# Channel attention: the reciprocal of the softmax sums as ScalarE's exp(-ln) and one Newton step on VectorE

## The chip, the cores and the metric

The kernel runs on one core of one Trainium2 chip. Times are device microseconds (us) of one execution of the whole program. The program is four transformer layers over a batch of 4 sequences of 512 tokens with 128 features. The change touches one stage of the fourth layer, called the channel stage here.

## The reference, cut to the changed stage

For each token, 16 heads take their 64 channels as a sequence of length 64: scores are products of single numbers, a causal mask lies over them, and a softmax runs over the channels. What the change touches is the division inside `softmax`.

```python
Q = (x @ Wq + bq).reshape(b, s, H, C) * inv_sqrt_c        # H = 16, C = 64
K = (x @ Wk + bk).reshape(b, s, H, C)
V = (x @ Wv + bv).reshape(b, s, H, C)
scores = jnp.einsum('bshq,bshk->bshqk', Q, K)
mask = jnp.triu(jnp.ones((C, C), dtype=bool), 1)
scores = jnp.where(mask, -jnp.inf, scores)
w = jax.nn.softmax(scores, axis=-1)
attn = jnp.einsum('bshqk,bshk->bshq', w, V)
return attn.reshape(b, s, HID) @ Wo + bo
```

The result is added to x and normalised, and then goes to a router and to experts.

## The kernel before

A first loop over the 4 sequences does three layers, expert blocks follow, then a second loop over the 4 sequences does the channel stage, and last come the experts of layer four. In the channel stage a sequence is 4 tiles (`tt`, 0 to 3) of 128 tokens. A tile's scores are cut into `NC` = 18 chunks (`c`, 0 to 17) of up to 128x1536 numbers: 6 `early` ones for the upper half of the queries (`half` = 1), then 8 `rect` and 4 `late` ones for the lower half (`half` = 0). All engines walk through the 72 chunks `n` in an order written out by hand, held together by semaphores.

A chunk goes through these steps. GpSimd multiplies queries and keys into one of five buffers `D3` (L1662). VectorE subtracts the maxima (`subtract`, L1712), two chunks ahead of its own `weigh`. ScalarE takes exp in place (L1631). TensorE adds up the numbers over the keys with transposing matmuls into the PSUM bank `psD[half]`, the softmax's denominators (`sum_chunk`, L1530). VectorE multiplies by the values into `W3` (`weigh`, L1726). TensorE adds those up into `psA[half]`, the numerators (L1530 again), one chunk later.

The 8 lowest queries of each head ("own" scores) go another way: ScalarE does them with 128 short exps a tile, 9 or 10 after each chunk from c = 1 to 14 (`own_scores`, L1621). The first of a tile waits until TensorE has finished the last own sums of the tile before, `own_num` (L1539). Their sums come at the end of a tile: TensorE's `own_den` at c = 15 and 16, VectorE's multiplication (L1732) at c = 16 and 17, TensorE's `own_num` at c = 17 and at c = 0 of the next tile.

`finish(tt, half)` on VectorE divides: a reciprocal of `psD[half]` (L1740), then a product with `psA[half]` into `AT` (L1746), 128x512 each. It is called for half 1 at c = 8 of the same tile (`FINISH_1`), and for half 0 at c = 3 of the next tile (`FINISH_0`), or at the stage's end for the last tile. TensorE projects `AT` at c = 6 of the next tile. For tiles 0 to 2, TensorE fills the next tile's keys and queries at c = 8 to 11 (`fill_qk`, L1499 and L1500), and ScalarE moves each part one chunk later (`move_qk`, L1603 and L1607). At c = 12 VectorE scans the next tile's keys (L1685), and the maxima of the next tile follow at c = 14 and c = 0 (L1698 to L1700).

Of the kernel before, what the change touches and what calls it, by code (L numbers as in the profile page):

```python
# [10 lines left out]
ALU = mybir.AluOpType  # L11
ACT = mybir.ActivationFunctionType
# [3 lines left out]
BATCH, T = 4, 512  # L16
NT = T // P
# [48 lines left out]
def transformer(nc, inp, out, last_stage=8):  # L66
    ctx = ExitStack()
    with ctx:
        def sb(name, cols, rows=P, dtype=FP32):
            return ctx.enter_context(nc.sbuf_tensor(name, [rows, cols], dtype))  # L70
# [3 lines left out]
        def sem(name):  # L74
            s = ctx.enter_context(nc.semaphore(name))
            sems.append(s)
            return s
# [20 lines left out]
        wa2 = sb("wa2", 3 * NH * HD)  # L98
# [32 lines left out]
        tab = sb("tab", 2 * BLOCKS_2, dtype=U32)  # L131

        gb, xb = wq1, wk1

        rows_d = nc.dram_tensor("rows_d", ((NE + 1) * REGION, ROW), FP32, kind="Internal").ap()
        y2_d = nc.dram_tensor("y2_d", ((NE + 1) * REGION, P), FP32, kind="Internal").ap()
# [8 lines left out]
        def take(cols):  # L145
            a = arena[:, top[0]:top[0] + cols]
            top[0] += cols
            assert top[0] <= AR + LENT, top[0]
            return a
# [76 lines left out]
        RD = QN  # L226
        AT = [take(NH * HD) for _ in range(2)]
# [9 lines left out]
        rows = take(16)  # L237
# [232 lines left out]
        def route_sems(name):  # L470
# [10 lines left out]
        both = sem("both")  # L481
        pr_ = {k: sem(f"prune_{k}") for k in ("s0", "sc", "ff", "bias", "w", "step")}
        c3 = {k: sem(f"c3_{k}") for k in (
            "d", "e", "w", "den", "num", "attn", "proj", "qk", "qk_sb", "v", "kh", "prod", "chain", "rows",
            "own", "own_den", "own_w", "own_num", "q_ps", "neg")}

        def x_ready(eng, stage):
# [16 lines left out]
        def of_tile(a, i):  # L504
            return a[:, i * P:(i + 1) * P]
# [29 lines left out]
        def back_act(act, j, k, i, bank):  # L535
            n = nrm
            act.wait_ge(n["xps"], NT * j + k + 1)
            nc.scalar.activation(of_tile(xT, i), psum[:, bank, 0:P], ACT.Copy).then_inc(n["xT"], 1)  # L538
# [667 lines left out]
        def scatter_pool(pool, k):  # L1206
            nc.gpsimd.indirect_dma_start(out=rows_d[:, :], out_offset=bass.IndirectOffsetOnAxis(ap=place[:, k:k + 1], axis=0),
                                         in_=xrow[:, k * ROW:(k + 1) * ROW], in_offset=None).then_inc(scattered, 16)
# [226 lines left out]
        psA = [psum[:, 4, :], psum[:, 5, :]]  # L1435
        psD = [psum[:, 6, :], psum[:, 7, :]]
        scratch = psum[:, 2, :]
        HB_ = NH * HD // 2
        NC = len(chunks)
        NALL = NT * NC  # L1440
        EARLY, LATE = len(early), len(early) + len(rect)
# [7 lines left out]
        SCAN, MAX_1 = EARLY + 6, EARLY + 8  # L1449
        V0_AT = NC - 1  # L1450

        SCATTER_AT = {EARLY + k: k for k in range(NT)}
        GATHER_AT = {EARLY + k: k for k in range(PLACES)}

# [5 lines left out]
        PARTS, PART = 4, HD // 4  # L1460
# [21 lines left out]
        def qk_bank(tt, j):  # L1482
            return psum[:, (4, 5, 3, 2)[j], :] if tt == 0 else scratch
# [111 lines left out]
        def channel_act(act):  # L1595
            s = c3

            def move_qk(tt, j):
                dst = (K3, Q3)[j // 2][tt % 2]
                act.wait_ge(s["qk"], 4 * tt + j + 1)  # L1600
                if tt >= 2:
                    act.wait_ge(s["prod"], (tt - 1) * NC)
                nc.scalar.activation(dst[:, j % 2 * 512:j % 2 * 512 + 512], qk_bank(tt, j), ACT.Copy,  # L1603
                                     scale=HD ** -0.5 if j < 2 else 1.0).then_inc(s["qk_sb"], 1)
                if j < 2:
                    by_head = KH[tt % 2].rearrange("p (h c) -> p c h", h=NH)[:, j * HD // 2:(j + 1) * HD // 2, :]
                    nc.scalar.activation(by_head, qk_bank(tt, j).rearrange("p (c h) -> p c h", h=NH), ACT.Copy, scale=HD ** -0.5)\  # L1607
                        .then_inc(s["kh"], 1)

            def own_scores(tt, c):  # L1610

                by_key = EA.rearrange("p (k n) -> p k n", k=HD)
                keys = KH[tt % 2].rearrange("p (h k) -> p h k", h=NH)
                if c == min(OWN_AT):
                    act.wait_ge(s["kh"], 2 * tt + 2)
                    act.wait_ge(s["neg"], tt + 1)
                    if tt > 0:
                        act.wait_ge(s["own_num"], tt * PARTS)
                for r, h in OWN_AT[c]:
                    j = r * NH + h  # L1620
                    nc.scalar.activation(by_key[:, 0:HD - r, j], keys[:, h, 0:HD - r], ACT.Exp, bias=NB[:, j:j + 1],  # L1621
                                         scale=Q3[tt % 2][:, j:j + 1]).then_inc(s["own"], 1)

            for j in range(4):
                move_qk(0, j)
            act.wait_ge(s["qk_sb"], 4)
            for n in range(NALL):
                tt, c = n // NC, n % NC
                cols = chunks[c].cols
                act.wait_ge(s["d"], n + 1)  # L1630
                nc.scalar.activation(D3[n % 5][:, 0:cols], D3[n % 5][:, 0:cols], ACT.Exp).then_inc(s["e"], 1)  # L1631
                if c == Q0_AT and tt + 1 < NT:
                    act.wait_ge(s["qk_sb"], 4 * tt + 8)
                    act.wait_ge(s["d"], (tt + 1) * NC)
                    nc.scalar.activation(psM[0], Q3[(tt + 1) % 2][:, 0:HB_], ACT.Copy).then_inc(s["q_ps"], 1)
                if tt + 1 < NT and c in MOVE_AT:
                    move_qk(tt + 1, MOVE_AT[c])
                if c in OWN_AT:
                    own_scores(tt, c)
                if c == ROWS and tt > 0:  # L1640
                    act.wait_ge(s["proj"], tt)
                    nc.scalar.activation(of_tile(rT, tt - 1), scratch[:, 0:P], ACT.Copy).then_inc(s["rows"], 1)
            for tt in range(NT):
                back_act(act, 1, tt, tt, tt % 2)

        def channel_pool(pool):
            s = c3
            for n in range(NALL):
# [14 lines left out]
                last.then_inc(s["prod"], 1)  # L1663
                if tt == 0 and c in SCATTER_AT:
                    scatter_pool(pool, SCATTER_AT[c])
                if tt == 1 and c in GATHER_AT:
# [3 lines left out]
        def channel_dve(dve):  # L1670
            s = c3
            chain = [0]

            def then(ins):

                chain[0] += 1
                ins.then_inc(s["chain"], 1)
                dve.wait_ge(s["chain"], chain[0])
# [54 lines left out]

            def finish(tt, half):

                done = tt * NC + (EARLY if half == 1 else NC)
                dve.wait_ge(s["den"], done)
                if half == 0:
                    dve.wait_ge(s["own_den"], (tt + 1) * PARTS)
                then(nc.vector.reciprocal(RD, psD[half]))  # L1740
                dve.wait_ge(s["num"], done)
                if half == 0:
                    dve.wait_ge(s["own_num"], (tt + 1) * PARTS)
                if tt >= 2:
                    dve.wait_ge(s["proj"], tt - 1)
                nc.vector.tensor_tensor(AT[tt % 2][:, half * HB_:(half + 1) * HB_], RD, psA[half], ALU.mult)\  # L1746
                    .then_inc(s["attn"], 1)
                dve.wait_ge(s["attn"], 2 * tt + 2 - half)

# [5 lines left out]
            for n in range(NALL):  # L1755
                tt, c = n // NC, n % NC
                if tt > 0:
                    if c == MAX_0:
                        maxima(tt, 0)
                    if c == FINISH_0:  # L1760
                        finish(tt - 1, 0)
                    if c == STATS:
                        dve.wait_ge(s["rows"], tt)
                        stats_dve(dve, 1, tt - 1, tt - 1, of_tile(rT, tt - 1))
                    if c == SCALE:
                        scale_dve(dve, 1, tt - 1, tt - 1, of_tile(rT, tt - 1))
                if c == FINISH_1:
                    finish(tt, 1)
                if tt + 1 < NT:
                    if c == SCAN:  # L1770
                        scan_keys(tt + 1)
                    if c == MAX_1:
                        maxima(tt + 1, 1)
                if n + 2 < NALL:
                    subtract(n + 2)
                weigh(n)
            finish(NT - 1, 0)
            dve.wait_ge(s["proj"], NT)
            stats_dve(dve, 1, NT - 1, NT - 1, scratch[:, 0:P])
# [124 lines left out]
        with nc.Fori(0, BATCH) as b:  # L1904
            with nc.Block() as block:
# [14 lines left out]
                @block.scalar  # L1920
                def _(act):
                    norm_act(act, 0, (3, 4))
                    channel_act(act)
                    route3_act(act)
# [97 lines left out]
```

## Time and profile before

| | us |
|---|---|
| median of 3 runs | 3361.55 |
| lowest, highest | 3359.6, 3368.39 |
| the profiled execution | 3359.82 |
| its span on the core | 3357.6 |

The profile is of one execution. Each instruction has a start, a duration, and, where its engine sat idle before it, the idle time with the instruction that ended it. The four passes of the channel stage lie between 1565 and 3240 us of the span; nearly all that is read here is from the first of them, and the others repeat it. In the tables of the trace PE is TensorE, DVE VectorE, ACT ScalarE and POOL GpSimd.

### The profile page before, as it was taken

What the parts mean: (1) busy time and instruction counts of PE and PEld (TensorE: products, weight loads), DVE (VectorE), ACT (ScalarE), POOL (GpSimd) and SP (SyncE); (2) the same over time, 40 slices, a digit from 0 to 9 for tenths busy, and PEclk for the clock granted to TensorE, in tenths of its full rate; (3) what the DMA queues carried; (4) which work ended last, traced back from release to release, by engine and by line L of the source; (5) the groups of instructions that cost most, each with busy time, mean ns of one, the idle gap of its engine ahead of it and who ended that gap; (6) DMA issues with size and microseconds to landing.
All of it is one profiled execution on the core that took longest, in us unless ns stands there. A gap on an engine that the chain in (4) does not pass through costs nothing. (4 is left out here: it accounts for less than half of the span.)

```text
span 3357.6 us, 53815 instructions
## 1 busy us (share of the span) xinstructions
PE 2734.4 (81%) x19496; PEld 2117.8 (63%) x19496; DVE 2228.7 (66%) x4199; ACT 1853.3 (55%) x4363; POOL 1544.6 (46%) x1473
## 2 busy tenths in 40 slices
PE   1998699869986998596888878888788887788857
PEld 0465546554655575495777766777677776677756
DVE  2167416842683268433999959999599995999943
ACT  0364436543554455422887718877287773877723
POOL 0141214221422241313886618767088761886614
PEclk8999899989998999898999989999799998999988
DMA  9400000000000000093000000000000000000005
GB/s 221 132 1 1 5 10 1 1 5 10 1 1 5 10 1 1 21 332 104 4 7 1 1 5 4 7 1 1 5 4 7 1 1 5 4 7 1 1 19 162
DMA packets 75396, 93.46 MB, mean 28 GB/s; under 512 B 9324, under 2 KB 61339, under 8 KB 74984
## 3 DMA queue, kind: packets, MB, share of 16 engines
q1 hardware_dynamic: 61278, 70.70, 7.5%
q0 software_dynamic: 5184, 10.29, 0.9%
q10 hardware_dynamic: 8650, 8.77, 0.8%
q8 instruction: 167, 2.74, 0.3%
q14 instruction: 117, 0.96, 0.1%
HBM read 61.58 MB, written 28.62 MB: 27 GB/s over the span
## 5 line engine op out<-in xcount | busy, mean ns | idle before, releaser
L1662 POOL TENSOR_TENSOR arena<-arena 128x1536 f32<-128x1536 f32 (+9 forms) x480 | 1024.5, 2161 | 337.0 <-DVE arena L1726 250.1
L1530 PE MATMUL psum<-ident,arena 128*128 128x128 f32 (+7 forms) x7168 | 869.0, 279 | 221.7 <-ACT arena L1631 204.0
L1530 PEld LDWEIGHTS psum<-ident,arena 128*128 128x128 f32 (+7 forms) x7168 | 792.2, 137 | 328.4 <-ACT arena L1631 260.6
L1621 ACT ACTIVATE arena<-arena 128x64 f32<-128x64 f32 (+7 forms) x2048 | 707.7, 484 | 144.1 <-PE psum L1539 144.1
L1726 DVE TENSOR_TENSOR arena<-arena,psum 128x1536 f32<-128x1536 f32 (+9 forms) x480 | 494.3, 1062 | 78.2 <-ACT arena L1631 70.5
L1712 DVE TENSOR_TENSOR arena<-arena,psum 128x1536 f32<-128x1536 f32 (+9 forms) x480 | 493.6, 1061 | 22.6 <-POOL arena L1662 20.7
L894 POOL TENSOR_SCALAR arena<-arena 128x512 f32<-128x512 f32 (+3 forms) x512 | 264.1, 533 | 498.7 <-DVE arena L857 498.6
L1631 ACT ACTIVATE arena<-arena 128x1536 f32<-128x1536 f32 (+2 forms) x288 | 405.7, 1415 | 148.9 <-DVE arena L1712 148.9
L815 ACT ACTIVATE arena<-arena 128x512 f32<-128x512 f32 (+3 forms) x512 | 281.7, 552 | 183.5 <-DVE arena L850 183.5
L517 POOL TENSOR_SCALAR veps<-mv 128x1 f32<-128x1 f32 x112 | 21.5, 192 | 707.7 <-DVE mv L512 703.0
L768 PEld LDWEIGHTS psum<-ident,arena 128*128 128x128 f32 x1280 | 142.1, 144 | 169.5 <-ACT arena L826 83.6
L768 PE MATMUL psum<-ident,arena 128*128 128x128 f32 x1280 | 186.1, 287 | 70.8 <-ACT arena L826 41.7
L1539 PE MATMUL psum<-ident,arena 128*128 128x128 f32 (+7 forms) x2048 | 234.0, 273 | 0.0
L1539 PEld LDWEIGHTS psum<-ident,arena 128*128 128x128 f32 (+7 forms) x2048 | 223.4, 137 | 1.2
L497 PE MATMUL psum<-ident 128*128 128x128 f32 x976 | 143.4, 297 | 65.8 <-issue 39.4
L726 PE MATMUL psum<-arena 64*128 64x256 f32 (+3 forms) x1024 | 187.7, 472 | 10.0 <-DVE arena L850 8.1
L850 DVE CUSTOM_DVE_ANT_0 arena<-psum,cmask 128x384 f32<-128x384 f32 (+3 forms) x256 | 112.0, 488 | 120.0 <-PE psum L726 120.0
L497 PEld LDWEIGHTS psum<-ident 128*128 128x128 f32 x976 | 136.9, 216 | 75.3 <-issue 69.2
L784 PE MATMUL psum<-arena 128*64 128x128 f32 x2560 | 180.5, 282 | 0.4
L538 ACT ACTIVATE xT<-psum 128x128 f32<-128x128 f32 x112 | 29.8, 277 | 241.4 <-PE psum L533 241.4
L784 PEld LDWEIGHTS psum<-arena 128*64 128x64 f32 x2560 | 138.4, 138 | 29.9 <-issue 28.0
L850 DVE CUSTOM_DVE_ANT_0 arena<-psum,arena 128x512 f32<-128x512 f32 (+3 forms) x256 | 112.3, 488 | 53.9 <-PE psum L726 32.6
(265 smaller groups left out, 3796.7 us busy)
## 6 DMA issues: line engine op xcount, KB each, us to landing
arena<-in_L_ffn_W SPq DMA_DIRECT2D x39, 768.0 KB
arena<-in_L_ffn_W SPq DMA_DIRECT2D x23, 514.0 KB
rows_d<-xrow SPq DMA_DIRECT2D x1, 9504.0 KB, 51.0
y_d<-xrow SPq DMA_DIRECT2D x1, 9216.0 KB, 80.5
arena<-rows_d SPq DMA_DIRECT2D x62, 66.0 KB, 3.9
y_d<-arena POOLq DMA_DIRECT2D x39, 64.0 KB, 4.8
arena<-in_L_ffn_h_w ACTq DMA_DIRECT2D x2, 1024.0 KB
wa<-in_L_attn_W_attn ACTq DMA_DIRECT2D x1, 1536.0 KB
```

What stands on the lines that cost most here:

```text
L497: nc.tensor.matmul(psum[:, bank, 0:P], ident[:], ident[:], start=True, stop=True)
L768: last = nc.tensor.transpose(GX[:, half, c:c + P], two(PRG[b % 4])[:, half, c:c + P], ident[:])
L784: last = nc.tensor.matmul(bank[half * HD:(half + 1) * HD, j * P:(j + 1) * P], V[:, c:c + HD], pt[:, half, j * g.n + kt * P:j * g.n + (kt + ...
L815: nc.scalar.activation(pr, pr, ACT.Exp, bias=nb[:, u:u + 1], scale=-1.0, accum_out=rsum[:, u:u + 1]).then_inc(s["probs"], 1)
L894: nc.gpsimd.tensor_scalar(pr, pr, rinv[:, u:u + 1], 1.0, ALU.mult, ALU.mult).then_inc(s["scaled"], 1)
L1530: last = nc.tensor.matmul(ps[ch.half][0:rows, to:to + P], buf[:, c:c + rows], ident[:], start=first, stop=False, is_transpose=True, skip_g ...
L1539: last = nc.tensor.matmul(ps[0][0:rows, 0:P], EA[:, k * NH * OWN:k * NH * OWN + rows], ident[:], start=False, stop=k == HD - 1, is_transpo ...
L1621: nc.scalar.activation(by_key[:, 0:HD - r, j], keys[:, h, 0:HD - r], ACT.Exp, bias=NB[:, j:j + 1], scale=Q3[tt % 2][:, j:j + 1]).then_inc( ...
L1631: nc.scalar.activation(D3[n % 5][:, 0:cols], D3[n % 5][:, 0:cols], ACT.Exp).then_inc(s["e"], 1)
L1662: last = nc.gpsimd.tensor_tensor(of_piece(D3[n % 5], piece), q, keys_on(K3[tt % 2], k, nk, w), ALU.mult)
L1712: last = nc.vector.tensor_tensor(d, d, queries_on(psM[ch.half], ch, piece), ALU.subtract)
L1726: last = nc.vector.tensor_tensor(of_piece(W3[n % 2], piece), of_piece(D3[n % 5], piece), keys_on(psV, k, nk, w), ALU.mult)
```

## The change

ScalarE gets a new step, `seeds(tt, half)`. It waits for the denominators to be complete, writes ln of `psD[half]` (128x512) into a buffer `RS[half]`, which lies in `wa2` (weights of layer three, not used any more), and then exp of minus that in place. For half 1 this stands after the own scores of c = 7 of the same tile (`SEED_1`), for half 0 after the own scores of c = 1 of the next tile (`SEED_0`), and after the last chunk for the last tile. VectorE's `finish` has no reciprocal any more. It waits for the seed r, makes d times r, then (that minus 2) times r, which is the negative of Newton's next value, and takes the sign back in the product with `psA[half]`, which becomes a scalar_tensor_tensor. Nothing else is changed.

```diff
+        SEED_1, SEED_0 = EARLY + 1, 1
...
+            def seeds(tt, half):
+                act.wait_ge(s["den"], tt * NC + (EARLY if half == 1 else NC))
+                if half == 0:
+                    act.wait_ge(s["own_den"], (tt + 1) * PARTS)
+                k = 2 * tt + 2 - half
+                if k >= 3:
+                    act.wait_ge(s["attn"], k - 2)
+                nc.scalar.activation(RS[half], psD[half], ACT.Ln).then_inc(s["ln"], 1)
+                act.wait_ge(s["ln"], k)
+                nc.scalar.activation(RS[half], RS[half], ACT.Exp, scale=-1.0).then_inc(s["seed"], 1)
...
                 if c in OWN_AT:
                     own_scores(tt, c)
+                if c == SEED_1:
+                    seeds(tt, 1)
+                if c == SEED_0 and tt > 0:
+                    seeds(tt - 1, 0)
...
+            seeds(NT - 1, 0)
             for tt in range(NT):
                 back_act(act, 1, tt, tt, tt % 2)
...
             def finish(tt, half):
                 done = tt * NC + (EARLY if half == 1 else NC)
-                dve.wait_ge(s["den"], done)
-                if half == 0:
-                    dve.wait_ge(s["own_den"], (tt + 1) * PARTS)
-                then(nc.vector.reciprocal(RD, psD[half]))
+                dve.wait_ge(s["seed"], 2 * tt + 2 - half)
+                then(nc.vector.tensor_tensor(RD, psD[half], RS[half], ALU.mult))
+                then(nc.vector.scalar_tensor_tensor(RD, RD, -2.0, RS[half], ALU.add, ALU.mult))
                 dve.wait_ge(s["num"], done)
...
-                nc.vector.tensor_tensor(AT[tt % 2][:, half * HB_:(half + 1) * HB_], RD, psA[half], ALU.mult)\
+                nc.vector.scalar_tensor_tensor(AT[tt % 2][:, half * HB_:(half + 1) * HB_], RD, -1.0, psA[half], ALU.mult, ALU.mult)\
                     .then_inc(s["attn"], 1)
```

What the build makes of `seeds` the diff does not tell. This is the order of ScalarE's instructions around c = 7 and 8 of a sequence's first tile, before the change (the 128x1536 rows are the exps of chunks, the short ones own scores):

```order
L1631 ACTIVATE arena<-arena 128x1536
L1621 ACTIVATE arena<-arena 128x61 x10
L1631 ACTIVATE arena<-arena 128x1536
L1621 ACTIVATE arena<-arena 128x60 x9
L1631 ACTIVATE arena<-arena 128x1536
```

And with the change (L1647 and L1624 are the old L1631 and L1621):

```order
L1647 ACTIVATE arena<-arena 128x1536
L1624 ACTIVATE arena<-arena 128x61 x10
L1636 ACT_TABLE_LOAD
L1636 ACTIVATE wa<-psum 128x512
L1638 ACT_TABLE_LOAD
L1638 ACTIVATE wa<-wa 128x512
L1647 ACTIVATE arena<-arena 128x1536
L1624 ACTIVATE arena<-arena 128x60 x9
L1647 ACTIVATE arena<-arena 128x1536
```

Four instructions now stand between the own scores of c = 7 and the exp of c = 8: besides ln and exp two loads of ScalarE's function tables, one ahead of each. The same four stand at all eight places of a sequence.

VectorE's order around c = 8 of the same tile, before (the last row is the `subtract` that follows):

```order
L1726 TENSOR_TENSOR arena<-arena,psum 128x1536
L1740 RECIPROCAL arena<-psum 128x512
L1746 TENSOR_TENSOR arena<-arena,psum 128x512
L1712 TENSOR_TENSOR arena<-arena,psum 128x1536
```

And with the change (L1747 and L1733 are the old L1726 and L1712):

```order
L1747 TENSOR_TENSOR arena<-arena,psum 128x1536
L1760 TENSOR_TENSOR arena<-psum,wa 128x512
L1761 SCALAR_TENSOR_TENSOR arena<-arena,wa 128x512
L1767 SCALAR_TENSOR_TENSOR arena<-arena,psum 128x512
L1733 TENSOR_TENSOR arena<-arena,psum 128x1536
```

Three instructions stand where two stood; no other instruction of VectorE has moved, and TensorE's and GpSimd's orders are as they were.

## Rows read from the trace of the kernel before

**Rows 1.** Busy time of each engine over the span, from the page.
```profile
PE 2734.4 (81%) x19496; PEld 2117.8 (63%) x19496; DVE 2228.7 (66%) x4199; ACT 1853.3 (55%) x4363; POOL 1544.6 (46%) x1473
```

**Rows 2.** Stretches: start:end, length, busy us (x instructions) by engine, granted TensorE clock, DMA share, GB/s.
```profile
1780.30:1827.20 46.90, 39.56 (x291) 31.68 (x289) 40.99 (x41) 46.39 (x107) 35.81 (x15) 1.00 0.00 1
1827.20:1850.00 22.80, 17.27 (x122) 14.97 (x123) 22.70 (x17) 20.36 (x45) 13.73 (x6) 0.93 0.00 1
1850.00:1874.40 24.40, 24.40 (x211) 22.66 (x210) 24.33 (x24) 3.97 (x4) 14.93 (x12) 1.00 0.01 1
```

**Rows 3.** ScalarE in order of time: start, duration, instruction, [idle before <- releaser].
```profile
1780.29 3.15 ACT L1621 ACTIVATE arena<-arena 128x64 f32<-128x64 f32 x9 [12.81 <-PE psum L1539]
...
1806.00 3.44 ACT L1621 ACTIVATE arena<-arena 128x61 f32<-128x61 f32 x10
...
1815.76 0.60 ACT L1603 ACTIVATE arena<-psum 128x512 f32<-128x512 f32 x1 [0.51 <-PE psum L1500]
...
1874.45 3.16 ACT L1621 ACTIVATE arena<-arena 128x64 f32<-128x64 f32 x9 [12.00 <-PE psum L1539]
```

**Rows 4.** VectorE in order of time, second tile to third; last row, the first tile.
```profile
1784.79 1.82 DVE L1726 TENSOR_TENSOR arena<-arena,psum 128x896 f32<-128x896 f32 x2 [1.89 <-ACT arena L1631]
...
1806.12 1.75 DVE L1726 TENSOR_TENSOR arena<-arena,psum 128x1536 f32<-128x1536 f32 x1 [0.78 <-ACT arena L1631]
1807.80 3.35 DVE L1740 RECIPROCAL arena<-psum 128x512 f32<-128x512 f32 x1
...
1821.55 1.75 DVE L1726 TENSOR_TENSOR arena<-arena,psum 128x1536 f32<-128x1536 f32 x1 [0.84 <-ACT arena L1631]
...
1827.20 1.75 DVE L1726 TENSOR_TENSOR arena<-arena,psum 128x1536 f32<-128x1536 f32 x1 [2.23 <-ACT arena L1631]
...
1640.48 1.75 DVE L1726 TENSOR_TENSOR arena<-arena,psum 128x1536 f32<-128x1536 f32 x1 [1.00 <-ACT arena L1631]
```

**Rows 5.** ScalarE around a table load in the first loop, in order of time.
```profile
167.20 2.11 ACT L802 ACTIVATE arena<-psum 128x512 f32<-128x512 f32 x5 [0.26 <-PE psum L708]
169.33 1.28 ACT L815 ACT_TABLE_LOAD   x1
```

**Rows 6.** Groups by line and shape: xcount, busy us, mean ns, idle before.
```profile
L1603 ACT ACTIVATE arena<-psum 128x512 f32<-128x512 f32 x64 | 38.0, 594 | 45.3 <-PE psum L1500 45.2
L1740 DVE RECIPROCAL arena<-psum 128x512 f32<-128x512 f32 x32 | 107.2, 3350 | 0.0
L1746 DVE TENSOR_TENSOR arena<-arena,psum 128x512 f32<-128x512 f32 x32 | 22.0, 687 | 17.8 <-PE psum L1539 16.8
L1056 DVE SCALAR_TENSOR_TENSOR arena<-psum,s,arena 128x512 f32<-128x512 f32 x16 | 12.0, 751 | 22.7 <-PE psum L1009 22.7
```

**Rows 7.** One line of ScalarE: durations in ns, least, median and most.
```profile
L1635 ACT ACTIVATE psum<-arena x12: 574/582/586, 1663.5 to 3123.9; 128x512 f32<-128x512 f32 x12
```

**Rows 8.** TensorE in order of time; first three rows channel stage, last one the first loop.
```profile
1807.15 2.78 PE L1530 MATMUL psum<-ident,arena 128*128 128x128 f32 x24
1810.97 2.84 PE L1530 MATMUL psum<-ident,arena 128*128 128x128 f32 x24 [1.03 <-ACT arena L1631]
...
1827.22 4.51 PE L1530 MATMUL psum<-ident,arena 128*128 128x128 f32 x24 [0.90 <-ACT arena L1631]
...
303.10 1.97 PE L768 MATMUL psum<-ident,arena 128*128 128x128 f32 x8 [3.46 <-POOL arena L894]
```

**Rows 9.** Two stretches, columns as in rows 2: after that 3.46 us wait, and inside the 4.51.
```profile
303.10:305.10 2.00, 2.00 (x10) 1.67 (x10) 1.90 (x5) 0.02 (x1) 0.62 (x1) 0.50 0.00 0
...
1828.00:1829.00 1.00, 1.00 (x7) 1.00 (x6) 1.00 (x2) 1.00 (x5) 0.00 (x0) 0.50 0.00 0
```

**Rows 10.** The stage's end in the first sequence: TensorE's last own_den; VectorE's last finish.
```profile
1945.37 3.66 PE L1539 MATMUL psum<-ident,arena 128*128 128x128 f32 x32
...
1951.72 3.35 DVE L1740 RECIPROCAL arena<-psum 128x512 f32<-128x512 f32 x1
1959.28 0.69 DVE L1746 TENSOR_TENSOR arena<-arena,psum 128x512 f32<-128x512 f32 x1 [4.21 <-PE psum L1539]
```

More of the change, by code:

```diff
@@ L133, in transformer @@
         gb, xb = wq1, wk1
+        RS = [wa2[:, 4 * T + j * T:4 * T + (j + 1) * T] for j in range(2)]
         rows_d = nc.dram_tensor("rows_d", ((NE + 1) * REGION, ROW), FP32, kind="Internal").ap()
@@ L483, in transformer @@
         c3 = {k: sem(f"c3_{k}") for k in (
-            "d", "e", "w", "den", "num", "attn", "proj", "qk", "qk_sb", "v", "kh", "prod", "chain", "rows",
+            "d", "e", "w", "den", "num", "attn", "proj", "seed", "ln", "qk", "qk_sb", "v", "kh", "prod", "chain", "rows",
             "own", "own_den", "own_w", "own_num", "q_ps", "neg")}
```

## The prediction, made before the changed kernel ran

> **What bounds the kernel now.** I read the busy times first, then stretches of one tile, then each engine in order of time. Over the span TensorE leads with 81% and VectorE has 66%, ScalarE 55% [rows 1], which would make a move of work from VectorE to ScalarE look right. The span is not one stage, though. One tile of the channel stage runs from the first own score at 1780.29 to that of the next tile at 1874.45, 94.2 us [rows 3]. Its three stretches differ [rows 2]. In the first 46.9 us ScalarE is busy 46.39, VectorE 40.99. In the next 22.8 VectorE is busy 22.70. In the last 24.4 TensorE (24.40) and VectorE (24.33) are full and ScalarE has 3.97.
>
> The loop that closes around a tile is this. Own scores wait for the last `own_num` of the tile before (12.0 and 12.8 us of idle ScalarE) [rows 3]; from there ScalarE runs exps and own scores without a pause but for 0.51 us, and VectorE's `weigh` waits for it again and again, 1.89, 0.78, 0.84 and 2.23 us [rows 4]. The last of these, at 1827.20, is chunk 11. After it VectorE has scans, maxima and own products and never waits again before the tile ends. So a tile costs ScalarE's time up to the exp of chunk 11, then VectorE's and TensorE's time. What ScalarE is given between c = 1 and c = 11 lengthens the tile by all of it; what VectorE is spared there turns into more waiting. Both seeds (c = 1 and c = 7) and both finishes (c = 3 and c = 8) lie in that stretch.
>
> **The removed work.** A finish is 3.35 + 0.69 = 4.04 us now [rows 6]. Afterwards it is a product, two scalar_tensor_tensor, each 128x512: 0.69 by the product's row and 0.75 by the nearest scalar_tensor_tensor's [rows 6], about 2.2 us. VectorE is spared 1.9 us, 32 times, 59 us in all. At the stage's end the reciprocal is already covered: after it VectorE waits 4.21 us for TensorE's sums [rows 10]. Elsewhere VectorE waits for ScalarE right after a finish's neighbours [rows 4]. I take 0 for the gain. Were this cover gone, it would be at most 59 us.
>
> **The added work on ScalarE.** The order has four instructions per seed. A table load took 1.28 us, starting 0.02 after the end of five ACTIVATEs run together [rows 5]. Ln reads a PSUM bank into SBUF like L1603, 0.594 us, and exp of 128x512 is near L1635's 0.582 [rows 6, 7]. Two neighbouring ACTIVATEs overlap by about 0.1 us and a load takes that away once, which adds 0.1, and the gaps are 4 x 0.02. Sum: 2 x 1.28 + 0.594 + 0.582 + 0.1 + 0.08 - 0.1 (exp overlaps its successor) = 3.82 us. Bounds: 3.6 if gaps and overlaps vanish, 4.1 if the chained exp needs 0.3 for its semaphore; the second load stands ahead of that wait and covers it, so I take 3.82.
>
> How many of the 8 seeds of a sequence lie on the path: in the first tile `weigh` of chunk 11 also waits for ScalarE (1.00 us [rows 4]), so its seed counts; tiles two, three and four have two each. That is 7. The last stands behind the last chunk: TensorE's `own_den` ends at 1949.0, the seed would be ready near 1952.9, VectorE ends its own product at 1951.7 and its last product cannot start before 1959.3 [rows 10]. Hidden, with 4.9 us to spare after the two Newton steps. So 4 x 7 x 3.82 = 107 us.
>
> Of a table load the Trainium skill ("ScalarE: Activation LUTs", "What ACT_TABLE_LOAD costs") says that a switch also drains the engine for 1.38 us, 2.66 in all. The row has no such gap; by the page the sum would be 28 x 2 x 1.38 = 77 us larger. The row is the nearer witness. The same page ("Table sets: the hidden batching unit") says that ln followed by exp costs one load, as one set holds both. By that rule a seed would cost 2.5 us and the sum 70 us. The order of this build has two loads, so the rule does not hold here.
>
> **The added wait on TensorE.** Behind a seed stand the exp of c = 8 (or c = 2), and `move_qk`. TensorE waits 1.03 us for the exp of c = 8 now [rows 8] and would wait 4.85. After a wait of 3.46 us in the first loop the granted clock was 0.50, the 1.2 GHz level, and 8 matmuls took 1.97 us [rows 8, 9]. In the channel stage the clock also falls now and then: the 24 matmuls of a chunk's two sums took 4.51 us instead of 2.84, with the clock at 0.50 inside [rows 8, 9]. If it falls behind the seed of c = 7, these 24 matmuls are late by 4.51 - 2.84 = 1.67 us; `fill_qk` stands behind them, and ScalarE, which already waits 0.51 us for it [rows 3], waits that much longer. It has keys and queries to move in tiles one to three, so 4 x 3 x 1.67 = 20 us. Bounds: 0, if the clock holds or other dips go away in exchange; 28 x 1.67 = 47 if every seed pays it. At c = 2 there is no move and VectorE has the spared 1.9 us in hand, so I take 20.
>
> **The sum.** 3359.82 + 107 + 20 = 3487 us. The profiled execution is 1.7 us under the median of 3361.55, less than runs differ among themselves, so I predict 3488 for the median. A difference of 0.3%, 10 us, is about what a measurement of this kernel tells from none.
>
> **Rivals.**
> (a) The clock costs nothing: 3359.8 + 107 = 3467. For it: the 28 seeds hold TensorE up at moments where its work is short, and dips that exist today may only move. Against it: a wait as long as the new ones was followed by a low clock.
> (b) The clock costs more: up to 3359.8 + 107 + 47 = 3514, and 3530 if the 2.1 us of `fill_qk` also run slow some of the times.
> (c) Faster: VectorE is the bound of the stage and ScalarE has room. Then 28 finishes give 28 x 1.9 = 53 us, 3307. It decides when ScalarE's free time in the stretch of the seeds reaches 3.8 us for each. The stage as a whole speaks for it (VectorE full for 47 of 94 us), the first stretch against it: ScalarE idles 0.51 us of 46.9 there [rows 2, 3].
> (d) Each load holds ScalarE for 2.7 us: ACTIVATEs in flight, more of them than in rows 5, must first leave. 107 + 28 x 2 x 1.38 = 184, so 3544 (3564 with the clock). That is the Trainium skill's drain, above. Rows 5 speak against it. With rows alone, a load after a busy engine is seen at 0.02 us of delay.
> (e) The loads are not both executed at full price, or half the delay is made good in the tile's second half, where fewer waits meet: 107 x 2/3 = 71, about 3431.
>
> **How the numbers follow.** Forecast with the clock term near 20 (3478 to 3500): 0.42. (a) 0.23. (b) 0.17. (c) 0.04. (d) 0.06. (e) 0.07, and 0.01 for seeds that are nearly hidden, without change. The range 3450 to 3530 takes in the forecast, (a) and (b), 0.82, and the 3.6 to 4.1 us of a seed (28 x 0.25 = 7 us either way). Leaving out (c), (d), (e) and no change leaves out 0.18. Faster by over 0.3%: 0.04. Within: 0.01. Slower: 0.95.
>
> **What the profile of the changed kernel would show.** ScalarE: 64 table loads more, at 1.28 us, and nothing but the four instructions between the own scores of c = 7 and the exp of c = 8, with 3.8 us from the one to the other. VectorE: three instructions near 0.7 us per finish, a wait for the seed before the one at c = 8 of about 5 us, and more idle time ahead of `weigh` in the first half of a tile. A tile of 94.2 us would be near 102 and, with the clock, 103.5. The second and third stretches of rows 2 would keep their lengths. TensorE: waits near 5 us after a seed, the clock below 1.00 behind them, and a `move_qk` at c = 9 that waits 2 us, not 0.5. I would be wrong if gaps stood around the loads (d), if ScalarE still idled before the tile's first own score by less than now by the amount of the seeds (c, e), or if the tile's tail grew.

## The result and the profile after

The changed kernel takes 3485.73 us (median of 4 runs, 3482.72 to 3490.45), against 3362.65 us for the kernel before. The ratio is 1.0362, with a 95% interval of 1.0343 to 1.0382: 3.6% slower. The forecast was 3488 us.

The engines' busy times, from the page of the changed kernel, to be set beside [rows 1]:

```profile
PE 2783.9 (80%) x19496; PEld 2165.3 (62%) x19496; DVE 2197.6 (63%) x4231; ACT 1976.5 (57%) x4491; POOL 1546.0 (44%) x1473
```

VectorE's busy time fell by 31.1 us and ScalarE's rose by 123.2. The span rose from 3357.6 to 3481.0, 123.4 us, nearly the same as ScalarE's 123.2. That the two agree to 0.2 us is partly luck: four of the 32 seeds do not lengthen the kernel, and other waits make up for them, as is added up further down.

Three stretches of the first sequence's third tile (start:end, length, busy us and instructions by engine, granted TensorE clock, DMA share, GB/s), cut at the same places as those of [rows 2]: from the first own score to the `weigh` of chunk 11 (at 1855.03), then to the late chunks, then to the next tile's first own score (at 1902.27).

```profile
1797.40:1855.00 57.60, 44.75 (x291) 36.76 (x289) 38.88 (x44) 54.05 (x115) 37.28 (x18) 0.88 0.00 1
1855.00:1877.80 22.80, 17.25 (x122) 14.95 (x123) 22.67 (x17) 20.37 (x45) 13.65 (x6) 0.93 0.00 1
1877.80:1902.20 24.40, 24.40 (x211) 22.66 (x209) 24.33 (x24) 3.98 (x4) 14.94 (x12) 1.00 0.01 1
```

The first stretch grew from 46.9 to 57.6 us. VectorE is busy for 38.9 us of it, where it was busy for 41.0, and the clock, 1.00 before, is 0.88. The two later stretches kept their lengths, 22.8 and 24.4 us, so the whole growth of the tile, 10.7 us, lies ahead of the `weigh` of chunk 11: two seeds of 3.9 us, and 2.9 us more of waiting at c = 9. ScalarE in order of time over the same tile (start, duration, instruction, idle before and its releaser), to be set beside [rows 3]:

```profile
1797.40 3.17 ACT L1624 ACTIVATE arena<-arena 128x64 f32<-128x64 f32 x9 [11.21 <-PE psum L1542]
...
1827.01 3.45 ACT L1624 ACTIVATE arena<-arena 128x61 f32<-128x61 f32 x10
1830.48 1.28 ACT L1636 ACT_TABLE_LOAD   x1
1831.78 0.60 ACT L1636 ACTIVATE wa<-psum 128x512 f32<-128x512 f32 x1
1832.39 1.28 ACT L1638 ACT_TABLE_LOAD   x1
1833.69 0.63 ACT L1638 ACTIVATE wa<-wa 128x512 f32<-128x512 f32 x1
1834.22 0.26 ACT L1662 ACTIVATE rT<-psum 128x128 f32<-128x128 f32 x1
...
1843.61 0.60 ACT L1606 ACTIVATE arena<-psum 128x512 f32<-128x512 f32 x1 [3.43 <-PE psum L1503]
...
1902.27 3.15 ACT L1624 ACTIVATE arena<-arena 128x64 f32<-128x64 f32 x9 [12.01 <-PE psum L1542]
```

The tile takes 104.9 us where it took 94.2 (the same tile in [rows 3]), the one before it 102.6 where it took 93.3. This tile is the longest of its kind: in the other three passes the third tile takes 102.5 to 102.7 us. A seed lasts from 1830.46, the end of the own scores, to 1834.32, and as its neighbours would have overlapped without it, it costs a little more: from the start of a block of nine own scores to the exp after it are 6.92 us with a seed between them (1797.40 to 1804.32) and 2.98 without (1805.70 to 1808.68), so 3.9. The fourth tile, which has two seeds and nothing to move, tells the same: from its first own score to the exp of chunk 11 it took 42.1 us (1874.45 to 1916.58) and takes 50.0 (1902.27 to 1952.23), 7.8 us more in each of the four passes. The wait of `move_qk` at c = 9 is 3.43 us, not 0.51. The last seed of a sequence is hidden, as its load starts after 11.34 us of idle ScalarE.

TensorE behind the seed of c = 7 of the second tile, and the clock there:

```profile
1733.36 4.16 PE L1533 MATMUL psum<-ident,arena 128*128 128x128 f32 x24 [4.93 <-ACT arena L1647]
```
```profile
1731.80:1736.00 4.20, 2.65 (x13) 2.65 (x14) 4.10 (x4) 4.20 (x11) 2.81 (x2) 0.61 0.05 16
```

It waits 4.93 us (4.85 were expected), and the clock is 0.61 in the mean from 1731.80 to 1736.00, so part of the 24 matmuls ran at the 1.2 GHz level: 4.16 us, not 2.84 [rows 8]. VectorE's three instructions and the moves on ScalarE, grouped by shape:

```profile
L1761 DVE SCALAR_TENSOR_TENSOR arena<-arena,wa 128x512 f32<-128x512 f32 x32 | 45.6, 1426 | 1.1
L1606 ACT ACTIVATE arena<-psum 128x512 f32<-128x512 f32 x64 | 37.9, 591 | 55.4 <-PE psum L1503 55.2
L1760 DVE TENSOR_TENSOR arena<-psum,wa 128x512 f32<-128x512 f32 x32 | 22.0, 688 | 78.2 <-ACT wa L1638 78.2
L1767 DVE SCALAR_TENSOR_TENSOR arena<-arena,psum 128x512 f32<-128x512 f32 x32 | 22.0, 687 | 20.5 <-PE psum L1542 19.6
```

VectorE waits 78.2 us for seeds. One row was not foreseen: the middle instruction of the Newton step, which reads two tiles of SBUF, took 1.43 us in the mean. In 24 of its 32 calls it took 0.69. In the first tile of each sequence it took 5.75 to 5.85, and once more per sequence 1.26 to 1.63.

### The profile page after: what moved, and what is told of

It is laid out like the page before. It is cut to its first block and busy times, and to the rows that moved or that the text cites. A ratio compares the mean times of both kernels' runs of the same rounds, so it can differ in the third digit from the quotient of the medians.

```text
span 3481.0 us, 54005 instructions
## 1 busy us (share of the span) xinstructions
PE 2783.9 (80%) x19496; PEld 2165.3 (62%) x19496; DVE 2197.6 (63%) x4231; ACT 1976.5 (57%) x4491; POOL 1546.0 (44%) x1473
## 5 line engine op out<-in xcount | busy, mean ns | idle before, releaser
L1533 PE MATMUL psum<-ident,arena 128*128 128x128 f32 (+7 forms) x7168 | 915.2, 289 | 296.0 <-ACT arena L1647 278.9
L1533 PEld LDWEIGHTS psum<-ident,arena 128*128 128x128 f32 (+7 forms) x7168 | 838.9, 143 | 401.5 <-ACT arena L1647 330.3
L1624 ACT ACTIVATE arena<-arena 128x64 f32<-128x64 f32 (+7 forms) x2048 | 707.2, 482 | 136.3 <-PE psum L1542 136.3
L1747 DVE TENSOR_TENSOR arena<-arena,psum 128x1536 f32<-128x1536 f32 (+9 forms) x480 | 494.5, 1063 | 150.0 <-ACT arena L1647 121.1
L1733 DVE TENSOR_TENSOR arena<-arena,psum 128x1536 f32<-128x1536 f32 (+9 forms) x480 | 493.7, 1062 | 22.4 <-POOL arena L1683 20.5
L1647 ACT ACTIVATE arena<-arena 128x1536 f32<-128x1536 f32 (+2 forms) x288 | 406.5, 1415 | 158.4 <-DVE arena L1733 158.4
L518 POOL TENSOR_SCALAR veps<-mv 128x1 f32<-128x1 f32 x112 | 21.5, 192 | 711.7 <-DVE mv L513 707.0
L1542 PE MATMUL psum<-ident,arena 128*128 128x128 f32 (+7 forms) x2048 | 234.0, 273 | 0.0
L1542 PEld LDWEIGHTS psum<-ident,arena 128*128 128x128 f32 (+7 forms) x2048 | 223.4, 137 | 1.2
L1753 DVE TENSOR_TENSOR arena<-arena,psum 128x2048 f32<-128x2048 f32 x64 | 143.2, 2278 | 2.9 <-PE psum L1542 2.9
```

Source lines behind the costliest of these rows:

```text
L1533: last = nc.tensor.matmul(ps[ch.half][0:rows, to:to + P], buf[:, c:c + rows], ident[:], start=first, stop=False, is_transpose=True, skip_g ...
L1542: last = nc.tensor.matmul(ps[0][0:rows, 0:P], EA[:, k * NH * OWN:k * NH * OWN + rows], ident[:], start=False, stop=k == HD - 1, is_transpo ...
L1733: last = nc.vector.tensor_tensor(d, d, queries_on(psM[ch.half], ch, piece), ALU.subtract)
L1747: last = nc.vector.tensor_tensor(of_piece(W3[n % 2], piece), of_piece(D3[n % 5], piece), keys_on(psV, k, nk, w), ALU.mult)
```

## The experiments

In the diffs, `-` is the changed kernel unless another is named.

**VectorE's part alone.**

```diff
-                if c == SEED_1:
-                    seeds(tt, 1)
-                if c == SEED_0 and tt > 0:
-                    seeds(tt - 1, 0)
...
-            seeds(NT - 1, 0)
...
-                dve.wait_ge(s["seed"], 2 * tt + 2 - half)
+                dve.wait_ge(s["den"], done)
+                if half == 0:
+                    dve.wait_ge(s["own_den"], (tt + 1) * PARTS)
```

> VectorE's part alone: ScalarE gives no seeds, finish waits for the denominators as before and does the three new instructions on whatever numbers stand in RS (left out: the seed, so the attention output is not the reference's). Theory of the prediction: what VectorE is spared in the first stretch of a tile only becomes waiting for ScalarE, so the time is that of before, 3362 us, within 0.3%. Rival (VectorE is the bound there): 28 finishes shorter by 1.9 us, minus the 24 us by which the changed trace shows the Newton step stretched, so 3309 to 3335 us.

Measured: 1.0088 of before (1.0070 to 1.0106), which is 30 us slower. (The medians, 3391.6 us against 3358.7, differ by 33, but that of this kernel counts one execution of 5112 us, which the ratio leaves out.) Neither theory said so: with nothing added on ScalarE, a step that was to be shorter made the kernel slower. In order of time, VectorE and then GpSimd in the first tile:

```profile
1625.83 0.68 DVE L1757 TENSOR_TENSOR arena<-psum,wa 128x512 f32<-128x512 f32 x1
1626.54 7.93 DVE L1758 SCALAR_TENSOR_TENSOR arena<-arena,wa 128x512 f32<-128x512 f32 x1
1634.51 0.69 DVE L1764 SCALAR_TENSOR_TENSOR arena<-arena,psum 128x512 f32<-128x512 f32 x1
```
```profile
1623.65 10.26 POOL L1678 TENSOR_TENSOR arena<-arena 128x1536 f32<-128x1536 f32 x3
```

The middle instruction ends at 1634.47, 0.56 us after GpSimd's three multiplications end at 1633.91. It starts while one runs and is not served between them. Over the sequence its calls took 7.93, 3.90, 4.20, 3.46, 0.69, 3.46, 0.69 and 0.69 us. The first own score of the second tile comes 131.3 us after the stage's table load where it came 122.3 us after it before, 9.0 us later, and the next two tiles are as long as before. So only the call of the first tile costs time, though the calls of 3.5 to 4.2 us are long too. In the four passes the first tile, from its first own score to that of the second, grew by 8.6, 9.2, 7.4 and 8.0 us, 33 us of the 35 by which the span grew. ScalarE pays for it at c = 10, where it waited 0.90 us before and now waits for TensorE's part of the next keys:

```profile
1645.27 0.60 ACT L1606 ACTIVATE arena<-psum 128x512 f32<-128x512 f32 x1 [6.77 <-PE psum L1503]
```

The instruction between SBUF and PSUM beside the stretched one is never stretched. On this the Trainium skill ("SBUF — State Buffer", "SBUF: two separate sides") says that VectorE and GpSimd share a pair of SBUF ports under an exclusive lock, held for a whole instruction, which VectorE also needs for two SBUF inputs while GpSimd reads SBUF. The trace agrees: 7.93 us beside GpSimd's multiplications, 0.69 us for the same call later in the sequence.

**The same with the product through PSUM.** This takes the suspected cause away.

```diff
-                then(nc.vector.tensor_tensor(RD, psD[half], RS[half], ALU.mult))
-                then(nc.vector.scalar_tensor_tensor(RD, RD, -2.0, RS[half], ALU.add, ALU.mult))
+                then(nc.vector.tensor_tensor(psD[half], psD[half], RS[half], ALU.mult))
+                then(nc.vector.scalar_tensor_tensor(RD, psD[half], -2.0, RS[half], ALU.add, ALU.mult))
```

> VectorE's part alone again, as in the run with the Newton step alone (left out: the seed), but d times r is written back to the PSUM bank, so that the scalar_tensor_tensor reads PSUM and SBUF, not two tiles of SBUF. Theory: the 33 us by which that run was slower are the 3.5 to 7.9 us that this instruction took while GpSimd multiplied; with a PSUM operand it takes 0.69 us each of 32 times and the time is that of before, within 0.3%. Rival 1 (the form with a scalar is stretched whatever it reads): 33 us slower again. Rival 2 (VectorE is the bound and its spared 62 us count): 3300 to 3330.

Measured: 1.0018 (1.0007 to 1.0030). The group by shape:

```profile
L1758 DVE SCALAR_TENSOR_TENSOR arena<-psum,wa 128x512 f32<-128x512 f32 x32 | 22.1, 692 | 1.1
```

No call is stretched and the loss of the run before is gone but for 0.2%, so the stretch was its cause. A finish costs VectorE 63 us less in this kernel: 32 x (4.04 - 2.07), by the two of [rows 6] and three of 0.69, and the time is no better than before. In the tiles two, three and four the way from the first own score to the exp of chunk 11 is as long as before, within 0.1 us (45.4, 45.4 and 42.1 us): VectorE waits instead, 87.5 us in all ahead of its `weigh` of 128x1536, where it was 49.9. That shows directly that VectorE's time in this stretch buys nothing there. In the four first tiles this way became 5.8 us shorter in all, and the rest of these tiles 9.7 us longer: VectorE's scan of the keys, which also reads two tiles of SBUF, took 8.8 to 9.0 us there in place of 6.7, while GpSimd multiplied back to back. The scan as the reason for the 9.7 us was not tested.

**ScalarE's part alone.**

```diff
-                nc.scalar.activation(RS[half], psD[half], ACT.Ln).then_inc(s["ln"], 1)
+                nc.scalar.activation(tiles(RS[half]), ones[:][:, None, :].to_broadcast([P, 4, P]), ACT.Ln).then_inc(s["ln"], 1)
...
-                dve.wait_ge(s["seed"], 2 * tt + 2 - half)
...
+                dve.wait_ge(s["den"], done)
+                if half == 0:
+                    dve.wait_ge(s["own_den"], (tt + 1) * PARTS)
+                then(nc.vector.reciprocal(RD, psD[half]))
...
```

> ScalarE's part alone: table load, ln, table load, exp stand at the eight places, but read a constant from SBUF and nobody reads their result; VectorE does the reciprocal and the product as before. Theory: the whole loss is ScalarE's, 28 x 3.91 = 109 us and the clock's part of about 11, so 3483 us like the changed kernel, within 8 us. Rival (finish's new wait for the seed is what costs, and ScalarE's time alone is partly hidden): clearly less, 3362 to 3440.

Measured: 1.0361 (1.0341 to 1.0382), the ratio of the changed kernel to the third digit. ScalarE's instructions alone make the whole loss. Neither the wait for the seed nor the stretched step adds to it. (Its ln, which reads SBUF, took 0.63 us, not 0.60, which is 1 us in all.)

**One table set.**

```diff
+            nc.scalar.preload_act_table_set("natural_log_exp_and_others")
             for j in range(4):
                 move_qk(0, j)
```

> The changed kernel with one table set that holds exp and ln, loaded once at the start of each sequence's channel stage, so that a seed is ln and exp alone. Theory: a seed falls from 3.91 to about 1.31 us, 28 x 2.6 = 73 us less, and TensorE waits near 2.3 us instead of 4.9 behind it, so the clock's 11 us go too: 3400 us, 3395 to 3415. Rival (the loads are hidden and the wait for the seed is what costs): above 3450.

Measured: 1.0211 (1.0191 to 1.0232), 3431 us. Better than the changed kernel by 1.5% of before, but 30 us short of the forecast. The stretched step is back: 2.88 us in the mean, 7.9 us in a first tile. Without the loads the seed comes earlier, and the step falls into GpSimd's multiplications again. As in the run with the Newton step alone, the first tiles pay: ScalarE waits 5.5 to 6.2 us at c = 10 there.

**One table set and the product through PSUM.** Both edits above.

> The kernel with one table set, loaded once a sequence, and the Newton step through PSUM. Theory: the two causes add up, a seed costs 1.31 us of ScalarE's time and the step no more waits for GpSimd, so 28 x 1.31 = 37 us over before, near 3396 to 3402; against 3431 with the step in SBUF. Rival (the table loads were not the larger part and the rest is the wait for the seed): it stays near 3430.

Measured: 1.0103 (1.0086 to 1.0120), 34.6 us over a before of 3356.18 us, where 28 x 1.31 = 37 was worked out. ScalarE in order of time:

```profile
1625.25 3.45 ACT L1624 ACTIVATE arena<-arena 128x61 f32<-128x61 f32 x10
1628.54 0.58 ACT L1636 ACTIVATE wa<-psum 128x512 f32<-128x512 f32 x1
1629.15 0.63 ACT L1638 ACTIVATE wa<-wa 128x512 f32<-128x512 f32 x1
1629.69 1.47 ACT L1648 ACTIVATE arena<-arena 128x1536 f32<-128x1536 f32 x1
```

From the start of the ten own scores to the exp are 4.44 us, with the loads 7.21 (1620.97 to 1628.18 in the changed kernel). So about 2.8 us of a seed are its loads. Before the change the same way took 3.30 us (1618.43 to 1621.73), so a seed without loads costs about 1.15 us and not 1.31, because it overlaps with its neighbours, and 28 of them cost 32 us. The fourth tile says the same: 44.4 us to the exp of chunk 11, not 42.1, for two seeds. So the sum of 37 was a little high; the 34.6 us are known to about 6, and do not tell the two apart.

**The product through PSUM in the changed kernel.** The same edit, with the seeds and their loads as they are.

> The changed kernel with the Newton step through PSUM and nothing else. Theory: behind the seeds with table loads GpSimd is mostly idle when the step comes, and the one that is stretched per sequence (5.8 us in the first tile) is hidden, so 3478 to 3486, no more than 0.2% under the changed kernel. Rival: the stretched steps cost their 24 us here too: 3460.

Measured: 1.0382 (1.0366 to 1.0398). The time lies in the range of the theory, 3482.9 us, and there is no gain: the ratio is, if anything, above the changed kernel's 1.0362, and the two intervals overlap. The stretch costs nothing where ScalarE is late by more.

**TensorE kept busy behind the seed, twice.**

```diff
+                if c == EARLY + 1:
+                    pe.wait_ge(s["d"], tt * NC + EARLY)
+                    if tt > 0:
+                        pe.wait_ge(s["rows"], tt)
+                    idle_work(2, 36)
                 if c in FILL_AT and tt + 1 < NT:
```

The copy of the rows is also issued ahead of the seed on ScalarE, so that the bank which the fill writes is free.

> The changed kernel with 36 idle matmuls (about 4.2 us) on TensorE at c = 7, where it otherwise waits 4.9 us for the exp behind the seed, and ScalarE's copy of the projected rows put ahead of the seed so that a bank is free. Theory: the granted clock stays at 1.00 there and move_qk at c = 9 waits 0.5 us again instead of 2.4, 1.8 and 3.4, so 11 to 24 us less than the changed kernel: 3462 to 3475. Rival (the longer move_qk waits have another cause, such as VectorE's late finish): no change, 3486.

Measured: 1.0405 (1.0387 to 1.0423). The fill was 72 instructions of 8.2 us in place of the 4.2 I had sized, so `fill_qk` came late for a reason of its own, and the time of this run says nothing on the clock. With 18 in place of 36:

> As the run with 36 idle matmul calls, which were 72 instructions and took 8.2 us, 4 us longer than the wait that they were to fill; now 18 calls, 36 instructions, 4.1 us. Theory: the 24 matmuls behind the seed of c = 7 take 2.84 us again, move_qk at c = 9 waits near 0.5 us, and the time is 11 to 24 us under the changed kernel, ratio to before 1.030 to 1.033. Rival (dips of the clock only move elsewhere, as in the longer fill, where the next dip came at c = 10): 0 to 8 us under it, ratio 1.034 to 1.036.

Measured: 1.0367 (1.0353 to 1.0382). TensorE in order of time, second tile:

```profile
1732.07 4.18 PE L498 MATMUL psum<-ident 128*128 128x128 f32 x36
1737.11 2.84 PE L1533 MATMUL psum<-ident,arena 128*128 128x128 f32 x24 [0.86 <-ACT arena L1652]
...
1747.72 2.84 PE L1533 MATMUL psum<-ident,arena 128*128 128x128 f32 x24 [1.18 <-ACT arena L1652]
...
1753.36 4.51 PE L1533 MATMUL psum<-ident,arena 128*128 128x128 f32 x24 [0.89 <-ACT arena L1652]
```

The 24 matmuls take 2.84 us again, and all twelve waits at c = 9 are 0.50 to 0.51 us, as in the theory. But now the 24 matmuls of c = 11 are slow (4.51 us), three chunks later, where in the changed kernel those of c = 8 and c = 10 were (4.16 and 4.41 us). The moves at c = 10 to 12 wait up to 5.33 us, 27.6 us in all where the changed kernel has 8.0, so over c = 9 to 12 the waits add up to 34 us, and to 36 in the changed kernel. The ratio lies just above the rival's range, and the rival is right in kind: the dip moved, and nothing was won.

**The seed of half 0 where ScalarE is idle.**

```diff
-                if c == SEED_0 and tt > 0:
+                if c == 0 and tt > 0:
                     seeds(tt - 1, 0)
```

> The changed kernel with the seed of half 0 after the exp of c = 0 of the next tile, not after the own scores of c = 1: ScalarE is idle there for 6.4 us and then 11 to 12 us more, outside the stretch that it bounds. Theory: 12 of the 28 seeds leave the path, 12 x 3.91 = 47 us less than the changed kernel, a ratio to before near 1.022. Rival (it is ScalarE's total time or the dip of the clock behind any seed that counts, not the place): ratio 1.034 to 1.038.

Measured: 1.0226 (1.0204 to 1.0248), 3440 us, where 1.022 was worked out. ScalarE in order of time between two tiles:

```profile
1680.21 1.28 ACT L1636 ACT_TABLE_LOAD   x1 [5.86 <-PE psum L1542]
...
1683.95 1.48 ACT L1647 ACTIVATE arena<-arena 128x1536 f32<-128x1536 f32 x1
1693.66 3.16 ACT L1624 ACTIVATE arena<-arena 128x64 f32<-128x64 f32 x9 [8.24 <-PE psum L1542]
```

The same four instructions stand between 5.86 and 8.24 us of idle time and cost nothing: from the exp of c = 0 to the first own score the second tile takes 20.8 us with them and without. The place of a seed decides its price.

**All three together**: one set, the product through PSUM, the early seed.

> One table set, the Newton step through PSUM, and the early seed of half 0. Theory: only 16 seeds of 1.31 us are left on the path, 21 us over before, ratio 1.006. Rival (VectorE's spared 62 us come to bear once ScalarE is hardly longer): at or below 1.000.

Measured: 1.0067 (1.0050 to 1.0084). It comes out as worked out, within the noise, and the spared VectorE time did not come to bear.

**Key moves on VectorE, in the kernel before.**

```diff
+            def move_keys(tt, j):
+                dve.wait_ge(s["qk"], 4 * tt + j + 1)
...
+                nc.vector.tensor_scalar(K3[tt % 2][:, j * 512:j * 512 + 512], qk_bank(tt, j), HD ** -0.5, None, ALU.mult)\
+                    .then_inc(s["qk_sb"], 1)
...
+                nc.vector.tensor_scalar(by_head, qk_bank(tt, j).rearrange("p (c h) -> p c h", h=NH), HD ** -0.5, None, ALU.mult)\
+                    .then_inc(s["kh"], 1)
...
                 weigh(n)
+                if tt + 1 < NT and MOVE_AT.get(c, 2) < 2:
+                    move_keys(tt + 1, MOVE_AT[c])
```

> The kernel before, its reciprocal kept, with the two key moves of c = 9 and 10 (two copies each out of PSUM) done by VectorE after its weigh of that chunk, not by ScalarE. It tests the claim on the bound by the other sign: work taken off ScalarE before chunk 11 shortens the tile. ScalarE sheds 2 x 1.37 us and the 0.51 us wait, 3.2 us, in tiles one to three; VectorE gets 2 x 1.7 us where it idles 5.7 us. Theory: 12 x 2 to 3.2 us = 24 to 39 us faster than before, ratio 0.988 to 0.993. Rival (VectorE is as much the bound there): 0.998 to 1.005.

Measured: 1.0089 (1.0073 to 1.0106), slower, against both. TensorE and then ScalarE in the second tile:

```profile
1742.80 1.12 PE L1499 MATMUL psum<-wk,xT 128*128 128x512 f32 x2 [2.16 <-DVE arena L1688]
1743.86 2.07 PE L1500 MATMUL psum<-bqkv,ones 1*128 1x512 f32 x2
1745.86 5.17 PE L1530 MATMUL psum<-ident,arena 128*128 128x128 f32 x24
```
```profile
1752.98 0.60 ACT L1603 ACTIVATE arena<-psum 128x512 f32<-128x512 f32 x1 [6.93 <-PE psum L1500]
```

From the second tile on, the keys and queries go through one PSUM bank, part by part. TensorE fills it again only once VectorE has emptied it, and VectorE comes to that after its `weigh`, so TensorE waits 2.16 us, its next 24 matmuls take 5.17 us, and ScalarE waits 6.93 for the third part. What ScalarE shed came back as a wait. The first half of the theory holds in this trace: from the first own score to the exp of chunk 11 tiles two and three take 42.1 us where they took 45.4, near the 3.2 us less that were worked out. The wait behind that exp, 6.9 us, and 11.1 to 11.5 us in the first tiles, takes it back and more. So the total says nothing on the bound, since the edit adds a chain of its own.

**Everything**: one set, the product through PSUM, the early seed and the key moves on VectorE, by the edits above.

> All together: one table set, Newton step through PSUM, early seed of half 0, and the key moves on VectorE, which has 1.9 us per finish to spare here. Theory: 21 us for the seeds of half 1, less 24 to 39 us for the moves, ratio 0.995 to 1.001, behind the kernel before with the key moves alone. Rival (with more room on VectorE the moves give more here): below 0.990.

Measured: 1.0031 (1.0019 to 1.0043), the fastest kernel with seeds and still not under the kernel before. Neither the theory's 0.995 to 1.001 nor the rival came out. With the seeds the key moves gave 0.4% more where they cost 0.9% without. The traces show where they differ: the wait for TensorE behind the exp of chunk 11, 6.93 us in the second tile above, is 3.48 us here:

```profile
1736.60 0.60 ACT L1606 ACTIVATE arena<-psum 128x512 f32<-128x512 f32 x1 [3.48 <-PE psum L1503]
```

That VectorE's shorter finish makes this difference was not tested by itself.

## Why the prediction was right

**What bounds.** Right, and shown from both sides: a VectorE that is spared 63 us gives no gain, and ScalarE's four instructions alone give 1.0361.

**The seed.** 3.82 us were worked out and 3.9 measured; ln took 0.597 and the loads 1.283 as in their rows, exp 0.63 where L1635's row, which writes PSUM, gave 0.58 [rows 7]. 28 on the path, one in eight hidden: 28 x 3.9 = 109 us, for 107. No gap stands around a load in the rows above (0.01 to 0.02 us), so rival (d) falls. The drain of 1.38 us with each load that the Trainium skill states ("ScalarE: Activation LUTs", "What ACT_TABLE_LOAD costs") is not seen in this trace.

**The clock.** The term was 20 us. At c = 9 the twelve waits add up to 27.6 us where twelve of 0.51 stood, 21.5 more, each behind a wait of TensorE of 4.9 to 5.7 us: the mechanism and its size, 20, were as forecast. But the waits at c = 10, the last that stand ahead of the exp of chunk 11, fell from 5.4 to 0.8 us, and behind that exp the tiles became 3.6 us shorter in all, as dips that stood at c = 12 before went away. What counts is 21.5 - 4.6 - 3.6 = 13 us, so the term was too large. Its weak step was "other dips go away in exchange", which I put at the edge of the term and not in its middle. At c = 2, where nothing is moved, the clock cost nothing: the fourth tile grew by two seeds and no more. The run with 18 idle calls shows that a dip can be moved and was not removed there.

**The sum.** Up to the exp of chunk 11 the sixteen tiles grew by 126.1 us in all, which is 109 for the seeds and 21.5 - 4.6 = 17 for the waits. Less the 3.6 behind it, and with another 2.6 us ahead of the stage, whose first table load comes at 1567.26 and not at 1564.69, that makes 125, and the span grew by 123.4. The 1.7 us between lie behind the last exps of the passes. The forecast growth of 127 us is 4 us above the span's: the seeds were 2 us too small, the clock 7 too large, and 1 us came from elsewhere. Part of the nearness is luck, as these have different signs.

**VectorE.** A finish was to take 2.2 us, and does in most cases, but the nearest row for the Newton step [rows 6] was one that reads PSUM, and the step reads two tiles of SBUF. The saving was 39.6 us in all, not 59. Here it was hidden, and the term of 0 for the gain was right. The time of that step should have been bounded by GpSimd's multiplication and not by 0.75 us. In a kernel with cheap seeds this error costs 36 us, the difference between 1.0211 and 1.0103.

## What to carry to other kernels

Read the stage, not the span: an engine with 55% of the whole can be the bound of the stretch in which its work is put, and the same four instructions cost 46 us over the kernel in one place and nothing in an idle stretch near it. Look in the built order for what an edit of one line makes of it; here the table loads, which the diff does not show, were 2.8 of the 3.9 us of a seed. An instruction that replaces another has to be compared by its operands too, since here the step with two SBUF inputs waited for GpSimd and the one with a PSUM input did not.

## What the runs showed of the hardware

A scalar_tensor_tensor of 128x512 with both tensors in SBUF took 0.69 us alone and up to 7.95 us while GpSimd ran its own multiplications of SBUF tiles back to back. In the call of 7.93 us it ended 0.56 us after the last of three, and was not let in between two. With the one tensor in PSUM it took 0.69 us in all of 32 calls. ScalarE's table load took 1.28 us each time, with 0.01 to 0.02 us on either side of it where ScalarE ran without a pause. A pair of loads added 2.8 us. The fall of TensorE's clock behind a wait near 5 us (24 matmuls in 4.16 us) could be kept away by filling the wait with 4.18 us of matmuls (2.84 us), but in the tile shown a fall came three chunks later (4.51 us), and the time was not better.
